# Routed expert weights kept on chip and addressed through a register, instead of streamed from HBM block by block

## The reference

```
def _L0_tok_ref(x, conv_w, conv_b):
    y = lax.conv_general_dilated(x, conv_w, ..., feature_group_count=C) + conv_b
    y = lax.reduce_window(y, jnp.float32(0.0), lax.add, (1, POOL, POOL, 1), (1, STRIDE, STRIDE, 1), 'VALID') / jnp.float32(POOL * POOL)
...
def _L0_ffn_ref(x, gate_w, gate_b, sw1, sb1, sw2, sb2, rw1, rb1, rw2, rb2):
    hs = jax.nn.gelu(jnp.einsum('td,nfd->ntf', t, sw1) + sb1[:, None, :], approximate=False)
    shared = jnp.einsum('ntf,ndf->td', hs, sw2) + sb2.sum(axis=0)
    logits = t @ gate_w.T + gate_b
    probs = jax.nn.softmax(logits, axis=-1)
    top_v, top_i = jax.lax.top_k(probs, K)
    cw = jnp.zeros_like(probs).at[jnp.arange(T)[:, None], top_i].add(top_v)
    hr = jax.nn.gelu(jnp.einsum('td,efd->etf', t, rw1) + rb1[:, None, :], approximate=False)
    oe = jnp.einsum('etf,edf->etd', hr, rw2) + rb2[:, None, :]
    routed = jnp.einsum('etd,te->td', oe, cw)
```

## Time and profile before

| | |
|---|---|
| device time, median of 3 runs | 2305.91 us (2300.82 to 2318.84) |
| the profiled execution | 2301.38 us |
| its span | 2299.2 us |
| PE, DVE, POOL, ACT busy | 1776.3, 1310.3, 955.7, 944.9 us |
| SP's transfers (queue q1) | 445.08 MB |

### The profile page before, as it was taken

How to read it: one execution, slowest core, us unless ns; L and a number is a source line. 1 busy time by engine, 2 the same in 40 slices (tenths; PEclk the granted TensorE clock), 3 DMA queues, 4 the chain that set the end, 5 groups by cost and what they waited for, 6 DMA issues and landing times.

```text
span 2299.2 us, 45631 instructions
## 1 busy us (share of the span) xinstructions
PE 1776.3 (77%) x14912; PEld 1412.5 (61%) x14912; DVE 1310.3 (57%) x3461; ACT 944.9 (41%) x2275; POOL 955.7 (42%) x770
## 2 busy tenths in 40 slices
PE   2364678897877888787878888878888898888757
PEld 2353666767666675666656576756756686666543
DVE  2664455666656666566656565556565665655332
ACT  1123435344443535345353534435353443536422
POOL 1233254453625454353545436244543525443222
PEclk9999779887978889688887978779796978899985
DMA  5566766666656566555756666566666657545320
GB/s 189 213 237 227 257 239 239 225 229 219 252 178 238 212 243 236 207 212 197 254 199 209 241 223 220 175 226 235 213 232 214 227 179 267 204 125 159 102 87 5
DMA packets 179421, 474.04 MB, mean 206 GB/s; under 512 B 21458, under 2 KB 95381, under 8 KB 162776
## 3 DMA queue, kind: packets, MB, share of 16 engines
q1 hardware_dynamic: 156688, 445.08, 54.4%
q0 software_dynamic: 8992, 19.42, 2.5%
q10 hardware_dynamic: 13480, 6.34, 1.0%
HBM read 439.37 MB, written 31.39 MB: 205 GB/s over the span
## 4 chain that ended last, share of the span: by engine, by line
PE 43%; DMA 23%; issue 12%; POOL 8%; SPq 5%; DVE 4%; another core or an unknown queue 2%; ACT 2%; ACTq 1%; POOLq 0%; DVEq 0%
DMA w_x<-in_w2x 11%; PE hid_bank L603 8%; DMA outs_d<-ys 6%; POOL yg L1337 5%; PE pool_bank L472 4%; DMA rows_d<-x2r,spot_i 3%; PE pool_bank L477 3%; PE hid_bank L592 3%; POOL xbuf L1326 2%; PE sec_bank L679 2%; PE sec_bank L622 2%; PE hid_bank L594 2%; DMA xbuf<-in_x 2%; PE sec_bank L639 2%
## 5 line engine op out<-in xcount | busy, mean ns | idle before, releaser
L1326 POOL TENSOR_TENSOR xbuf<-xbuf 128x512 f32<-128x512 f32 x256 | 339.4, 1326 | 769.3 <-DVE xbuf L1019 758.9
L848 ACT ACTIVATE hid<-hid_bank,w_x 128x128 f32<-128x128 f32 x960 | 272.7, 371 | 248.5 <-PE hid_bank L594 223.7
L592 PE MATMUL hid_bank<-xt,w_x 128*128 128x128 bf16 x960 | 195.9, 235 | 196.7 <-DMA w_x<-in_w2x 114.1
L603 PE MATMUL hid_bank<-w_x,hid 128*128 128x128 f32 x1920 | 319.8, 319 | 27.3 <-ACT hid L848 26.2
L603 PEld LDWEIGHTS hid_bank<-w_x,hid 128*128 128x128 f32 x1920 | 277.5, 222 | 59.1 <-ACT hid L848 35.5
L1019 DVE TENSOR_TENSOR xbuf<-xbuf 128x1536 f32<-128x1536 f32 x128 | 230.0, 1797 | 42.0 <-DMA xbuf<-in_x 41.8
L1179 DVE TENSOR_TENSOR ys<-hid_bank,w_x 128x128 f32<-128x128 f32 x240 | 67.9, 288 | 310.5 <-PE hid_bank L603 195.2
L592 PEld LDWEIGHTS hid_bank<-xt,w_x 128*128 128x128 bf16 x960 | 103.8, 108 | 217.3 <-DMA w_x<-in_w2x 179.4
L1040 DVE SCALAR_TENSOR_TENSOR taps<-pooled_s,tapw,taps 128x256 f32<-128x256 f32 (+1 forms) x416 | 214.7, 516 | 31.3 <-issue 24.6
L594 PE MATMUL hid_bank<-xt,w_x 128*128 128x128 bf16 x960 | 196.9, 236 | 0.0
L593 PE MATMUL hid_bank<-xt,w_x 128*128 128x128 bf16 x960 | 196.8, 236 | 0.0
(11 more groups left out here) (204 smaller groups left out, 3622.1 us busy)
## 6 DMA issues: line engine op xcount, KB each, us to landing
xbuf<-in_x SPq DMA_DIRECT2D x128, 2048.0 KB, 7.5
w_x<-in_w2x SPq DMA_DIRECT2D x240, 322.0 KB
w_x<-w_d SPq DMA_DIRECT2D x240, 256.0 KB
rows_s<-rows_d SPq DMA_DIRECT2D x48, 320.0 KB, 4.4
outs_d<-ys SPq DMA_DIRECT2D x240, 64.0 KB
out<-h ACTq DMA_DIRECT2D x16, 256.0 KB
hid<-in_w POOLq DMA_DIRECT2D x10, 256.0 KB, 4.2
rows_d<-x2r,spot_i POOLq DMA_INDIRECT x128
```

The lines of the kernel that those rows point to most:

```text
L592: nc.tensor.matmul(out_q, w1_x[:, k, 0, cols], high, start=True, stop=False)
L603: mm = nc.tensor.matmul(hid_bank[n % 2][:, 0:P], hid[:, n % RING, cols], w2_x[:, k, cols], start=q == 0, stop=q == FC - 1)
L848: ins = nc.scalar.activation(hid[:, n % RING, cols], hid_bank[n % 2][:, cols], ACT.Gelu, bias=w2_x[:, k, F + q:F + q + 1])
L1326: nc.gpsimd.tensor_tensor(v[:, :, 1, :], v[:, :, 1, :], v[:, :, 2 * k + 3, :], ALU.add) \
```

## The change

w1 of all experts stays where the setup puts it, in w1_b, and w2_s grows to all ten experts (2.5 MB of SBUF instead of 0.5). w1_x, w2_x, w1_d, the streams and the writes to w1_d are gone. PE reads a block's expert number into a register itself, ahead of `widen`'s waits, and keeps it for `narrow`; the weights' addresses are computed from it. The second bias comes by a matmul with a one-hot row (`owned`, a 24 x 15 table made by DVE, against three bfloat16 parts of the biases) at the start of `narrow`; the first bias comes from a table (`table`) that four small matmuls a group make in down_bank and ACT copies to bias_t. The rings xt and ys have five slots instead of three. hm shares h1's buffers.

```diff
-SLOTS = 3
+SLOTS = 5
...
-        w2_s = sb("w2_s", [P, NS, F])
-        w1_x = sb("w1_x", [P, SLOTS, 2, F], bf16)
-        w2_x = sb("w2_x", [P, SLOTS, F + FC + C])
+        w2_s = sb("w2_s", [P, NX, F])
+        bias_b = sb("bias_b", [P, F + C], bf16)
...
-                elif kind == "stream":
...
-                    e = eng.value_load(owner_i[b][0:1, j:j + 1], min_val=0, max_val=NE - 1)
-                    eng.dma_start(w1_x[:, k], w1_d[bass.ds(e, 1)].rearrange("e p h f -> (e p) h f")) \
-                       .then_inc(stream_in[k], 16)
-                    eng.dma_start(w2_x[:, k, :], w2x[bass.ds(e, 1)].rearrange("e p f -> (e p) f")) \
-                       .then_inc(stream_in[k], 16)
...
+            def table(g, b):
+
+                eng.wait_ge(gate_step, at(gate_step, g, 28))
+                if after(g, 1):
+                    eng.wait_ge(lift_ready, at(lift_ready, g - 1, NB))
+                for q in range(FC):
+                    mm = nc.tensor.matmul(down_bank[:, q * NB:(q + 1) * NB], bias_b[0:3 * NE, q * P:(q + 1) * P],
+                                          owned[b][0:3 * NE, :], start=True, stop=True)
+                mm.then_inc(table_done, 1)
...
-            def widen(g, j):
+            def widen(g, b, j):
 
                 n, k = NS * FC + j, j % SLOTS
-                eng.wait_ge(stream_in[k], at(stream_in[k], g, 32 * (j // SLOTS + 1)))
+                e = held[j] = eng.value_load(owner_i[b][0:1, j:j + 1], min_val=0, max_val=NE - 1)
                 eng.wait_ge(lift_ready, at(lift_ready, g, j + 1))
                 hid_free(g, n)
...
-                    nc.tensor.matmul(out_q, w1_x[:, k, 0, cols], high, start=True, stop=False)
-                    nc.tensor.matmul(out_q, w1_x[:, k, 1, cols], high, start=False, stop=False)
-                    mm = nc.tensor.matmul(out_q, w1_x[:, k, 0, cols], low, start=False, stop=True)
+                    w_high, w_low = (w1_b[:, bass.ds(e + NS, 1), h, cols].rearrange("p a f -> p (a f)") for h in range(2))
+                    nc.tensor.matmul(out_q, w_high, high, start=True, stop=False)
+                    nc.tensor.matmul(out_q, w_low, high, start=False, stop=False)
+                    mm = nc.tensor.matmul(out_q, w_high, low, start=False, stop=True)
...
-            def narrow(g, j):
+            def narrow(g, b, j):
...
+                e = held.pop(j, None)
+                if e is None:
+                    e = eng.value_load(owner_i[b][0:1, j:j + 1], min_val=0, max_val=NE - 1)
                 eng.wait_ge(hid_made, at(hid_made, g, n + 1))
+                nc.tensor.matmul(hid_bank[n % 2][:, 0:P], owned[b][0:3 * NE, j:j + 1].to_broadcast([3 * NE, P]),
+                                 bias_b[0:3 * NE, F:F + C], start=True, stop=False)
                 for q in range(FC):
-                    cols = slice(q * P, (q + 1) * P)
-                    mm = nc.tensor.matmul(hid_bank[n % 2][:, 0:P], hid[:, n % RING, cols], w2_x[:, k, cols],
-                                          start=q == 0, stop=q == FC - 1)
+                    w_q = w2_s[:, bass.ds(e + NS, 1), q * P:(q + 1) * P].rearrange("p a c -> p (a c)")
+                    mm = nc.tensor.matmul(hid_bank[n % 2][:, 0:P], hid[:, n % RING, q * P:(q + 1) * P], w_q,
+                                          start=False, stop=q == FC - 1)
...
                         ins = nc.scalar.activation(hid[:, n % RING, cols], hid_bank[n % 2][:, cols], ACT.Gelu,
-                                                   bias=w2_x[:, k, F + q:F + q + 1])
+                                                   bias=bias_t[:, q, j:j + 1])
...
+                    nc.vector.tensor_scalar(owned[b][:], owner[:], expert, None, ALU.is_equal).then_inc(gate_step, 1)
...
-                    nc.vector.tensor_tensor(ys[:, k, :], hid_bank[(NS * FC + j) % 2][:, 0:P], w2_x[:, k, F + FC:], ALU.add) \
-                      .then_inc(out_ready, 1)
+                    nc.vector.tensor_copy(ys[:, k, :], hid_bank[(NS * FC + j) % 2][:, 0:P]).then_inc(out_ready, 1)
```

All five lists of ORDER are written anew. SP's has no streams, and its x loads stand closer together. A part of PE's, before and after:

```diff
-        up.0 up.1 down.0 up.2 down.1 up.3 down.2 up.4 up.5 out' down.3 pool.0.0 pool.0.1 pool.0.2 down.4 up.6
-        down.5 up.7 down.6 pool.0.3 att.1 down.7 att.2 lift.0 widen.0 att.3 pre.2 lift.1 narrow.0 pre.3 lift.2
-        widen.1 pre.4 lift.3 widen.2 pool.1.0 pool.1.1 narrow.1 lift.4 att.4 narrow.2 pre.5 pre.6 pre.7 widen.3
+        up.0 up.1 table up.2 down.0 up.3 down.1 up.4 up.5 down.2 out' up.6 down.3 down.4 pool.0.0 pool.0.1
+        pool.0.2 up.7 down.5 down.6 att.1 down.7 att.2 lift.0 pool.0.3 lift.1 widen.0 widen.1 lift.2 att.3
+        narrow.0 pre.2 narrow.1 lift.3 widen.2 att.4 pre.3 lift.4 narrow.2 lift.5 pool.1.0 pre.4 pool.1.1 widen.3
```

166 lines of the change are left out of this document (89 added, 77 removed).

## The result

| | before | after |
|---|---|---|
| device time, median | 2303.36 us (2298.57 to 2318.84, 4 runs) | 2094.5 us (2071.78 to 2101.65, 4 runs) |
| ratio, with its 95% interval | | 0.9066 [0.8981, 0.9151] |
| the profiled execution | 2301.38 us | 2071.78 us |
| span less PE's busy time | 522.9 us | 324.3 us |
| mean granted clock | 0.85 | 0.925 |

The kernel is 9.3% faster. The forecast was 2193 us with a range of 2070 to 2390: the sign and the range held, and the gain was about twice the one forecast (209 us between the medians, not 110). The profiled execution is the fastest of the four, 22.7 us under the median; readings of its trace are set against 2188, the forecast's sum for the profiled execution. Of all executions reported here one is left out, the fourth of `load_narrow`: it took 3851.5 us, nearly double the other three.

A forecast was written before the change was run, and what follows sets the result against it. PE was taken as nearest the bound, running out of work at the weights' landing. 2301.4 - 145 - 60 - 25 + 21 + 96 = 2188 us for the profiled run, 2193 us as median; range 2070 to 2390.

The forecast's parts named there:

- What bounds the kernel: PE, 77% busy, runs out of work at widen: 114.1 us for weights' landing, 78.7 us through DVE's wait for stores.
- Part 1: Ahead of widen: without streams, three quarters of 192.8 us of idle PE goes, -145 us (-80 to -193).
- Part 3: Store, gather and mix at the group's turn: less traffic shortens landings, -25 us (0 to -70).
- Part 2: PE's clock: fewer stalls mean faster matmuls, 0.4 us per us of idle time, -60 us (0 to -149).
- Part 4: Added work: 240 bias matmuls 13 us, the table's matmuls 4 us, its ACT copies 4 us; +21 us.
- Part 5: Expert number loads and weight addresses on PE's sequencer in widen and narrow: 0.4 us a block, +96 us (0 to +372).
- Part 6: Start and new order of work (lifts further ahead, widen.0 widen.1 paired): charge 0, bounds +-30 us.
- B: Rival: PE's sequencer lead hides all the register work; 2097 us, chance 0.2.
- A: Rival: in widen and narrow the sequencer becomes PE's bound; slower, 2409 us at 1.3 us a block, chance 0.2.
- C: Rival: stalls move to the second layer's steps, halving parts 1 and 2; 2295 us, chance 0.15.
- The signs named in advance: Trace marks for parts 1, 2 and 5 and rivals A and C; a group over 131 us or under 117 refutes the forecast.

The follow-up runs named there:

- load_narrow: Changed kernel with the order of the kernel before; block j + 2's expert number is loaded right behind narrow j's float32 matmuls: 2025.07 us, ratio 0.8945.
- after_again: The changed kernel itself, unaltered, run again on the chip of the experiments: 2072.36 us, ratio 0.916.
- static: Changed kernel with fixed weight addresses (block j takes expert j % 8) and no registers on PE: 1986.26 us, ratio 0.8765.
- no_stream: Kernel before with only its first three weight streams; all blocks read those three slots: 2055.24 us, ratio 0.9065.
- old_order_3: Changed kernel with the order of the kernel before and three slots instead of five in xt and ys: 2151.05 us, ratio 0.9515.
- old_static: Changed kernel with the order of the kernel before, fixed weight addresses and no registers on PE: 2020.1 us, ratio 0.8927.
- no_bounds: Changed kernel with the order of the kernel before, the expert number loaded without its limits: 2294.62 us, ratio 1.0121.
- unread: Kernel before with all weight transfers still issued, but nobody waits for or reads them; PE takes fixed weights: 2104.95 us, ratio 0.9291.

## Why the prediction was right or wrong

**What bounds the kernel: right.** Taking the weights' landing away gave 159 us, and the store's stall came second. The landing was worth more than its 114.1 us of idle time, and the two slots 110 us, more than the 78.7 that the store's stall had.

**The sum against the two traces of one chip.** Forecast for the profiled execution 2188, measured 2071.8: 116 us too much.

| | forecast | measured |
|---|---|---|
| idle PE: parts 1 and 3 | -170 | -199 |
| clock: part 2 | -60 | some -165 |
| matmuls added: part 4 | +21 | some +70 |
| registers: part 5 | +96 | +65 |
| sum | -113 | -230 |

The first row is 522.9 - 324.3. The registers' row is PE's busy time in `after_again` less that in `static` (1742.2 - 1676.8), their idle time being equal; by the medians it is 86. The matmuls' row is an estimate from the distances of matmuls at full clock: 240 x 0.19 us within `narrow`, 21 us in all for the matmuls ahead of the bias matmul, and the forecast's own 4 for the table. The clock's row is what then remains of the change in busy time, -30.6 - 65 - 70, and is an estimate by as much.

**Part 2 is the term that failed most.** "I take 0.4 us per us": it was some 165/199 = 0.8 over the whole change, and where runs isolate a stall it is more, 64 to 78 us of busy time for 36 of idle time with the two slots. The 165 us lie beyond the forecast's upper end for this term, 149 us. The pair of windows it read the earlier trace rows gave one for one, and was marked down to 0.4 because a stall "can fall where the clock is low anyway"; no row was named for that discount, and the runs bear out little of it.

**Part 4 failed next, and hid half of it.** It took the 240 bias matmuls at "the size of L592, 0.056 us each". Each costs up to 0.29 us. The 100 us of busy time between `no_stream` and `old_order_3`, at one clock, agree: some 70 for the matmuls added, and the rest for registers, which cost 18 to 32 us of busy time in the old order with five slots. No run has the bias matmul alone, and why it is so dear stays open. That the sum missed by 116 us and not by more is luck: the clock was sized some 105 us too small and the matmuls some 50.

**Part 1 kept too little.** Three quarters of 192.8 us was kept for fear of the block's own chain. The idle time ahead of `widen` did fall by 162.9 us, more than the 145, and ahead of `narrow` (then "already" showing a wait for gelu) by 22.9 us in place of growing. Part 3 was wrong in its place: "less traffic shortens the landings", but the gathers wait 83.1 us for stores, 12 us more than before, as the store at the turn now lands behind a load of x (7.14 us for 2.63).

**Part 5, the registers: the size was right for this order, and it is not a constant.** 0.4 us a block was forecast, 0.36 was measured. From the load to the first address SP's row gave 0.57 us; PE's own operations add up to 0.47 us (0.301, 0.151, 0.018), and with the gaps between them it is 0.77 us (median of the trace). But the same operations cost 0.09 to 0.12 us a block in the old order, and nothing that can be told with the loads behind `narrow`. The working had the mechanism (the lead holds behind float32 work and not behind bf16 work) and the rivals named `widen` behind `widen`, but it charged an average instead of going through the list. It also took 12 addresses a `widen`; 8 were made. The matmuls stand 0.06 to 0.13 us apart, a little over the 0.06 to 0.09 forecast.

Whether a register makes the decoding of a matmul or of a weight load longer no row of before could show. The forecast worked out 1.2 us a block for that case from the Trainium skill ("TensorE: Matmul & The Clock Gate", section "Wait — 56ns, not 53.3ns?"). The page gives its 62 ns for a matmul; that a weight load would cost as much was the forecast's assumption. The trace doesn't agree with that case: the twelve matmuls from 1024.72 us on, their weights addressed by register, come 0.05 to 0.06 us apart, as the static ones of before did. In PEld's timeline,

```profile
1016.32 0.10 PEld L582 LDWEIGHTS hid_bank<-xt,w_b 128*128 x1 [0.56 <-issue]
1016.45 0.10 PEld L583 LDWEIGHTS hid_bank<-xt,w_b 128*128 x1
1016.46 0.10 PEld L584 LDWEIGHTS hid_bank<-xt,w_b 128*128 x1
```

L584, addressed by a register whose value is ready, follows L583 by 0.01 us. What shows is the time to make an address.

**Part 6, the order: "Charge 0" was no measure of it.** The new order gives 34 us without registers; with them it gives nothing, and loses 23 to 31 us against `after_again`. Its bounds of 30 just about hold. In the parts above it is the 25 us of idle time by which `static` stands under `old_static` (315.4 against 340.9), and the larger part of the registers' busy time.

**The rivals.** B's time, 2097, is almost the measured one, and B is refuted: `static` shows 68 to 86 us of registers not hidden. The errors of the other terms, the clock's above all, brought the sum there. A did not happen in this kernel, and `no_bounds` shows what it would have been: it costs 1.14 us a block more than `old_static` (274.5/240) and ends 1.2% above before; the point from which it decides is 1.0 us by these runs ((2261.4 - 2020.1)/240), and A had put it at 0.87, with 2409 us for 1.3 us a block. C's place grew, as it said, from 105.5 to 121.8 us ahead of pooling, with POOL at 10% of the chain. It took back 16 us and did not set the end. `static`, the fastest of all, has 126.5 us there.

**The signs named in advance.** q1 at 300.9 MB, no w_x in the chain, 33.8 us ahead of `widen` (under 50), clock 0.93 (0.87 or more), "issue" ahead of `widen` 18.4 us on PE and 58.4 on PEld (under 200): all as named. "No wait of L1179 for a store" held but for 9.9 of 102.3 us. A group of 115.9 us lies below the 117 that the forecast gave as its edge, and by that mark the forecast was wrong on the fast side.

**The way down, in one line each**, on the chips of the experiments: before 2264; nobody waits for the streams, 2105; no streams, 2055; registers, bias matmuls and table with three slots, 2151; five slots, 2041; the new order, 2072. The 96 us of the fourth step are 21 to 29 us of registers (measured with five slots) and, by the estimate, some 70 of matmuls.

## What to carry to other kernels

A stall of TensorE is worth more than its idle time if the clock goes down with it: here 36 us of idle time came with 64 to 78 us of slower matmuls, so price it from two stretches of the same work at either level and don't mark it down without a row. A register-addressed weight costs next to nothing by itself; loading the number and making the addresses is serial work of PE's sequencer, free behind a long float32 group (`load_narrow`) and paid in a bunch (6.4 us a group) or behind short matmuls, and the load's limits must stay, since without them every address is checked again. A small matmul put into a stream of larger ones is not priced by its own size: compare the distances of starts on both sides of it. An order of work that was good for another mix of costs is a change of its own: run it alone, with the new cost and without.

## What the runs showed of the hardware that was not expected

- PE's sequencer needs 0.30 us to load a number from SBUF, 0.15 for its check and 0.02 for the assertion; an address operation is recorded at 0.046 us, but where the sequencer has no lead, matmuls with one ahead of them come 0.12 to 0.13 us apart in place of 0.06. A weight load from a ready register follows after 0.01 us.
- A bf16 matmul of 24 rows and 128 columns costs far more than one of 128 rows: in after the next matmul starts 0.155 us behind it (median at full clock; 0.056 for L582 to L584 in `static`), and the bf16 matmul of 128 rows ahead of it takes 0.152 in place of 0.056. Few rows alone are not the cause: ahead of a matmul of 67 rows, in before as in after, it stays 0.056.
- An overloaded sequencer hides in the profile: in `no_bounds` PE is busy for 1973.1 us and idle for no more than in kernels 246 us faster, as each matmul's record (0.23 us) covers the gap of 0.20 us to the next. The distance of starts shows it; neither the busy share nor the idle time does.
- Transfers that nobody reads or waits for cost 50 us (`unread` against `no_stream`): 140 MB on the queue that the stores of ys share. Without them DVE's waits for those stores fell from 118.5 to 77.6 us.
